# Attention feature stages of a graph transformer: 64-row projections for pairs of token tiles, and column-tiled accumulations

## What is computed

```python
Q, K, V = heads(x @ Wq + bq), heads(x @ Wk + bk), heads(x @ Wv + bv)   # 16 heads of 64
Kp = relu(normalized(K) @ projection.T) + 0.1      # 256 features a head
Qp = relu(normalized(Q) @ projection.T) + 0.1
KV = einsum('bhsf,bhsd->bhfd', Kp, V)              # 256 x 64 a head
QKV = einsum('bhsf,bhfd->bhsd', Qp, KV)
normalizer = maximum(einsum('bhsf,bhf->bhs', Qp, sum_s(Kp)), 1e-6)
out = (QKV / normalizer) @ Wo + bo
```

## Time and profile before

| | |
|---|---|
| median of 3 runs | 3448.74 us (3441.88 to 3455.16) |
| profiled execution, its own time | 3453.75 us |
| span of its trace | 3452.0 us |
| mean granted TensorE clock | 0.941 |
| TensorE / VectorE / ScalarE / GpSimd busy | 90% / 61% / 37% / 12% |
| key stage | 299.3 to 442.3 us |
| query stage | 570.3 to 714.9 us, products until 721.8 us |

### The profile page before, as it was taken

The page is one execution under the profiler, slowest core; times in us unless marked ns, Lnnn a source line. Parts: engine busy times, 40 slices in busy tenths (PEclk is TensorE's granted clock), DMA queues, the critical chain, the costliest instruction groups (busy, mean ns, idle before and its releaser), DMA issues.

```text
span 3452.0 us, 52667 instructions
## 1 busy us (share of the span) xinstructions
PE 3101.3 (90%) x21876; PEld 2834.2 (82%) x21876; DVE 2116.8 (61%) x3710; ACT 1290.2 (37%) x2211; POOL 401.6 (12%) x302
## 2 busy tenths in 40 slices
PE   6999999989998799999489999989998999969992
PEld 6897797479987398888389997989998999968882
DVE  6985377977875744434556555776264734646664
ACT  4462055544421034333244334444044413325551
POOL 1044443442000100000300000000000000010002
PEclk9999999999998899999699999999999999969996
DMA  7322123122032156534641000452321432248777
GB/s 248 106 54 40 1 62 92 1 48 68 13 88 88 46 158 190 173 128 152 187 142 38 26 27 30 122 146 76 81 88 48 115 72 81 63 133 267 258 257 228
DMA packets 284267, 366.09 MB, mean 106 GB/s; under 512 B 52472, under 2 KB 234782, under 8 KB 282224
## 3 DMA queue, kind: packets, MB, share of 16 engines
q1 hardware_dynamic: 165035, 203.54, 20.0%
q0 software_dynamic: 51248, 68.03, 8.5%
q10 hardware_dynamic: 67717, 90.69, 8.1%
HBM read 285.75 MB, written 83.74 MB: 107 GB/s over the span
## 4 chain that ended last, share of the span: by engine, by line
PE 55%; DVE 4%; DMA 2%; ACT 2%; issue 1%; ACTq 1%; POOL 1%; POOLq 0%; DVEq 0%; SPq 0%
PE PV L459 12%; PE PV L460 12%; PE PV L461 12%; PE PV L563 6%; PE PS L459 3%; PE PS L461 3%; PE PS L460 3%; DMA b<-y_d,gidx 1%; PE PA L594 1%; PE PA L487 1%; DVE b L1848 1%; DVE b_split L1634 1%; ACTq L121 1%; ACT b L1248 1%; PE PA L878 1%
## 5 line engine op out<-in xcount | busy, mean ns | idle before, releaser
L459 PE MATMUL PV<-WH,b_split 128*125 128x256 f32 (+2 forms) x3708 | 1091.1, 294 | 124.6 <-DVE b_split L1634 107.7
L460 PE MATMUL PV<-WH,b_split 128*125 128x256 f32 (+2 forms) x3708 | 1077.4, 291 | 0.0
L461 PE MATMUL PV<-WH,b_split 128*125 128x256 f32 (+2 forms) x3708 | 1076.4, 290 | 0.0
L1634 DVE TENSOR_TENSOR b_split<-b,b_split 128x500 fp32r<-128x500 f32 x1040 | 687.4, 676 | 435.5 <-ACT b_split L1237 422.4
L1237 ACT CAST b_split<-b 128x500 fp32r<-128x500 f32 x1040 | 626.0, 612 | 808.8 <-PE PV L461 733.4
L459 PEld LDWEIGHTS PV<-WH,b_split 128*125 128x125 f32 (+2 forms) x3708 | 703.6, 190 | 149.7 <-issue 105.8
L460 PEld LDWEIGHTS PV<-WH,b_split 128*125 128x125 f32 (+2 forms) x3708 | 706.5, 191 | 9.9
L461 PEld LDWEIGHTS PV<-WH,b_split 128*125 128x125 f32 (+2 forms) x3708 | 703.0, 190 | 11.3
L1617 DVE TENSOR_TENSOR WH<-WS,WH 128x1024 fp32r<-128x1024 f32 x292 | 344.3, 1221 | 145.7 <-ACT WH L1222 144.4
L1222 ACT CAST WH<-WS 128x1024 fp32r<-128x1024 f32 x292 | 292.1, 1051 | 180.4 <-PE PV L563 143.4
L459 PE MATMUL PV<-b_split,WH 128*128 128x250 f32 (+3 forms) x1136 | 336.9, 297 | 9.2 <-DVE b_split L1634 6.4
(11 more groups left out here) (271 smaller groups left out, 3775.4 us busy)
## 6 DMA issues: line engine op xcount, KB each, us to landing
WS<-in_L_ffn_w SPq DMA_DIRECT2D x46, 1024.0 KB, 6.8
WH<-at_d SPq DMA_DIRECT2D x15, 1093.8 KB
WS<-in_L_ffn_gate_w SPq DMA_DIRECT2D x16, 1024.0 KB, 5.4
WS<-in_L_ffn_up_w SPq DMA_DIRECT2D x16, 1024.0 KB, 6.1
WS<-in_L_ffn_down_w SPq DMA_DIRECT2D x16, 1024.0 KB, 5.1
y_d<-b ACTq DMA_DIRECT2D x60, 256.0 KB
y_d<-b ACTq DMA_DIRECT2D x64, 196.0 KB
b<-key_d POOLq DMA_DIRECT2D x4, 2560.0 KB, 9.4
```

Of the source, the lines that this page charges most:

```text
L459: pe.matmul(o, a[0], b[0], start=start, stop=False, **kw)
L460: pe.matmul(o, a[0], b[1], start=False, stop=False, **kw)
L461: return pe.matmul(o, a[1], b[0], start=False, stop=stop, **kw)
L1634: ve.tensor_tensor(lo, src, hi.bitcast(F32), ALU.subtract).then_inc(xl_done, 1)
```

## The change

*Key stage.* An iteration handles two token tiles of a pair of heads (40 iterations instead of 80). For each tile and head one matmul of 64 rows (partitions 0 to 63 or 64 to 127) and 256 moving columns; a bank holds one head and both tiles. The matmuls that accumulate are the same ones, eight in an iteration; they follow one iteration behind.

*Query stage.* An iteration is a step. Four projections of 64 rows go to four banks, PV 0 to 2 and PS[2] (qf_bank). ScalarE alone empties them, with one Relu each (L1479 takes 0 as the bias), into columns 1 to cn of the features. The addition of 0.1 is gone: column 0 of each of the six feature buffers is set once to 0.1 by VectorE, so the matmul's first output column holds a tenth of the sum over the features of KV, which is what the addition would have added to every column. VectorE copies this pair of columns to tenths for the first chunk of a pair of heads and adds it in the two instructions that it keeps besides the reciprocal. The accumulations become eight of 64 columns of weights: part 0 makes the results of both heads, part 1 the normalizers, and head hh writes the output partitions from 64 hh, so results and normalizers of both heads stand in matching partitions. The copies of the normalizers between partitions (L1470, L1471) are gone, and one product serves both heads.

```diff
--- before.py
+++ after.py
@@ -238,6 +239,10 @@
         def q_feats(n):
 
             return RB[:, n % 6, :] if n % 6 < 4 else WHF[:, 1, UNIT + (n % 6 - 4) * HALF:UNIT + (n % 6 - 3) * HALF]
+
+        def qf_bank(k):
+
+            return PV[:, k, :] if k < 3 else PS[:, 2, :]
 
         def q_norm(step):
 
...
@@ -720,27 +724,36 @@
             pe.wait_ge(pt_in, 16)
             pe.wait_ge(ones_col, 1)
             mark["kp"] = v.n
-            for n in range(KD * NT + 2):
-                if n < KD * NT:
-                    pr, i = divmod(n, NT)
-                    if n == KD // 2 * NT:
+            for n in range(KD * NB + 1):
+                if n < KD * NB:
+                    pr, b = divmod(n, NB)
+                    if n == KD // 2 * NB:
                         pe.wait_ge(pt_in, 32)
-                    pe.matmul(v.take(pe)[0:R, :], cols(B3)[:, pr, i * R:(i + 1) * R], proj[pr],
-                              start=True, stop=True).then_inc(v_full, 1)
-                if n >= 2:
-                    m = n - 2
-                    pr, i = divmod(m, NT)
-                    pe.wait_ge(v_free, mark["kp"] + m + 1)
-                    if i == 0 and pr >= 2:
+                    banks = v.take(pe), v.take(pe)
+                    for t in range(2):
+                        i = 2 * b + t
+                        for hh in range(2):
+                            head = slice(hh * HD, (hh + 1) * HD)
+                            mm = pe.matmul(banks[hh][0:R, t * F0:(t + 1) * F0], cols(B3)[head, pr, i * R:(i + 1) * R],
+                                           proj[pr][head, hh * F0:(hh + 1) * F0], start=True, stop=True)
+                            if t == 1:
+                                mm.then_inc(v_full, 1)
+                if n >= 1:
+                    m = n - 1
+                    pr, b = divmod(m, NB)
+                    pe.wait_ge(v_free, mark["kp"] + 2 * (m + 1))
+                    if b == 0 and pr >= 2:
                         pe.wait_ge(kv_free, 2 * (pr - 1))
-                    for hh in range(2):
-                        at = i * NH + 2 * pr + hh
-                        for f in range(2):
-                            mm = pe.matmul(kv_acc(pr)[:, hh, f * P:(f + 1) * P].rearrange("p (c d) -> p c d", c=2),
-                                           RB[0:R, m % 4, hh * F0 + f * P:hh * F0 + (f + 1) * P],
-                                           v_heads[:, at:161:160 - at, :],
-                                           start=(i == 0 and f == 0), stop=(i == NT - 1),
-                                           skip_group_check=True)
+                    for t in range(2):
+                        i = 2 * b + t
+                        for hh in range(2):
+                            at = i * NH + 2 * pr + hh
+                            for f in range(2):
+                                mm = pe.matmul(
+                                    kv_acc(pr)[:, hh, f * P:(f + 1) * P].rearrange("p (c d) -> p c d", c=2),
+                                    RB[0:R, (2 * m + hh) % 4, t * F0 + f * P:t * F0 + (f + 1) * P],
+                                    v_heads[:, at:161:160 - at, :],
+                                    start=(i == 0 and f == 0), stop=(i == NT - 1), skip_group_check=True)
                     mm.then_inc(kp_used, 1)
             pe.wait_ge(kv_free, NH)
 
@@ -750,37 +763,39 @@
             turn_heads(2 * NQ * NB - 1)
             pe.wait_ge(s_free, s.n)
 
-            mark["qp"] = v.n
-            for n in range(NH * 6 + 4):
-                if n < NH * 6:
-                    step, hh, f = n // 4, n // 2 % 2, n % 2
-                    pr, c = divmod(step, 3)
+            for n in range(KD * 3 + 1):
+                if n < KD * 3:
+                    pr, c = divmod(n, 3)
                     c0, cn = CH[c]
-                    if n == NH * 3:
+                    if n == KD // 2 * 3:
                         pe.wait_ge(pt_in, 48)
-                    if f == 0:
-                        bank, done = v.take(pe), v_full
-                    else:
-                        if n >= 2:
-                            pe.wait_ge(qa_free, n // 2)
-                        bank, done = PS[:, 2, :], qa_full
-                    at = hh * F0 + f * P
-                    pe.matmul(bank[:, 0:cn], proj[pr][:, at:at + P], cols(B3)[:, pr, c0:c0 + cn],
-                              start=True, stop=True).then_inc(done, 1)
-                if n >= 4:
-                    m = n - 4
-                    step, hh, f = m // 4, m // 2 % 2, m % 2
-                    pr, c = divmod(step, 3)
+                    for f in range(2):
+                        if n >= 1:
+                            pe.wait_ge(qf_done, 4 * (n - 1) + 2 * (f + 1))
+                        for hh in range(2):
+                            head, at = slice(hh * HD, (hh + 1) * HD), hh * F0 + f * P
+                            pe.matmul(qf_bank(2 * f + hh)[:, 0:cn], proj[pr][head, at:at + P],
+                                      cols(B3)[head, pr, c0:c0 + cn], start=True, stop=True).then_inc(qf_full, 1)
+                if n >= 1:
+                    m = n - 1
+                    pr, c = divmod(m, 3)
                     cn = CH[c][1]
-                    if f == 0:
-                        pe.wait_ge(v_free, mark["qp"] + m // 2 + 1)
-                    else:
-                        pe.wait_ge(qa_done, m // 2 + 1)
-                    if m % 4 == 0 and step >= 2:
-                        pe.wait_ge(acc_free, 2 * (step - 1))
-                    pe.matmul(q_acc(step)[:, hh, 0:cn], KV[:, 2 * pr + hh, f, :], q_feats(m)[:, 0:cn],
-                              start=(f == 0), stop=(f == 1)).then_inc(qp_used, 1)
-            pe.wait_ge(acc_free, NH * 3)
+                    if m == 0:
+                        pe.wait_ge(tenths_ready, 6)
+                    if m >= 2:
+                        pe.wait_ge(acc_free, m - 1)
+                    for f in range(2):
+                        pe.wait_ge(qf_done, 4 * m + 2 * (f + 1))
+                        for part in range(2):
+                            for hh in range(2):
+                                at = (part + hh) % 2 * HD
+                                mm = pe.matmul(q_acc(m)[hh * HD:(hh + 1) * HD, part, 0:cn + 1],
+                                               KV[:, 2 * pr + hh, f, at:at + HD],
+                                               q_feats(4 * m + 2 * f + hh)[:, 0:cn + 1],
+                                               start=(f == 0), stop=(f == 1))
+                                if part == 1:
+                                    mm.then_inc(qp_used, 1)
+            pe.wait_ge(acc_free, KD * 3)
             linear_rows("wo0")
 
 
@@ -1451,7 +1466,7 @@
             head_pieces(0)
             for h in range(NH):
                 if h % 2 == 0:
-                    act.wait_ge(kp_used, NT * (h // 2 + 1))
+                    act.wait_ge(kp_used, NB * (h // 2 + 1))
                 kvp = kv_acc(h // 2)[:, h % 2, 0:2 * P].rearrange("p (f c d) -> p f c d", f=2, c=2)
                 dst = KV[:, h, :, :].rearrange("p f (c d) -> p f c d", c=2)
                 if h % 2 == 0:
@@ -1461,28 +1476,15 @@
                     act.copy(dst[:, :, 0, :], kvp[:, :, 1, :]).then_inc(kv_free, 1)
             head_pieces(NQ * NB)
 
-            def normalisers(step):
-
-                cn = CH[step % 3][1]
-                act.wait_ge(qp_used, 4 * (step + 1))
-                if step >= 2:
-                    act.wait_ge(acc_free, 2 * (step - 1))
-                act.copy(q_norm(step)[0:64, 0:cn], q_acc(step)[64:128, 0, 0:cn]).then_inc(den_done, 1)
-                act.copy(q_norm(step)[64:128, 0:cn], q_acc(step)[0:64, 1, 0:cn]).then_inc(den_done, 1)
-
-            for n in range(1, NH * 6, 2):
-                cn = CH[n // 4 % 3][1]
-                q = q_feats(n)[:, 0:cn]
-                if n >= 6:
-                    act.wait_ge(qp_used, n - 5)
-                act.wait_ge(qa_full, n // 2 + 1)
-                act.activation(q, PS[:, 2, 0:cn], ACT.Relu).then_inc(qa_free, 1)
-                act.wait_ge(qa_free, n // 2 + 1)
-                act.activation(q, q, ACT.Copy, bias=0.1).then_inc(qa_done, 1)
-                if n >= 7 and n % 4 == 3:
-                    normalisers((n - 7) // 4)
-            normalisers(3 * KD - 1)
-            act.wait_ge(acc_free, NH * 3)
+            for n in range(KD * 3):
+                cn = CH[n % 3][1]
+                for k in range(4):
+                    if k % 2 == 0:
+                        act.wait_ge(qf_full, 4 * n + k + 2)
+                        if 4 * n + k >= 6:
+                            act.wait_ge(qp_used, 4 * n + k - 4)
+                    act.activation(q_feats(4 * n + k)[:, 1:cn + 1], qf_bank(k)[:, 0:cn], ACT.Relu).then_inc(qf_done, 1)
+            act.wait_ge(acc_free, KD * 3)
             linear_residual(B1, A["x"])
 
 
@@ -1984,35 +1986,37 @@
 
             ve.wait_ge(table_zero, 16 * NZERO)
             head_pieces(0)
```

(40 more changed lines are left out.)

10 lines of the change are left out of this document (5 added, 5 removed).

## The result

The changed kernel takes 3396.45 us (median of 4 runs, 3393.57 to 3400.18); the kernel before took 3447.21 beside it (4 runs, 3441.88 to 3455.16). The ratio is 0.9851, with a 95% interval of 0.9832 to 0.987. That is 50.8 us less. The likeliest case of the prediction was 26.5 less (3422); 52 less (3397) was the rival *Full overlap*. So nearly twice the forecast gain came. The time lies inside the stated range.

The account below looks back on a forecast made before the run. TensorE was taken to bound the key stage alone and the query stage with VectorE nearly even. Key -9.6 and query -16.9 (matmuls -14.3, end -2.6) sum to -26.5 us: 3422 off the median; range 3378 to 3455.

Parts of the forecast that it names:

- likeliest case: Both stages: staggered overlap of array halves, switches of 0 to 0.28 us; sum 26.5 us less, 3422; chance 0.50.
- Full overlap: Rival, both stages: two heads' passes always run side by side; 52 us less, 3397; chance 0.18.
- What bounds the two stages: Key stage: TensorE alone; query stage: TensorE 5.6 us a step before, VectorE 5.2; after the change 5.3 against 4.1.
- Units of a pass: TensorE in both stages: a pass takes 0.22 us for 256 columns and 0.35 for 416.
- Switches: Both stages: each change of the array's shape costs 0.2 us, two per iteration or step; ends 0 and 0.28.
- the starts of the passes: Both stages: passes start staggered in program order; 5 units for eight projection passes, 9 for sixteen accumulation passes.
- The start of the query stage: Query stage, beyond its steps: 1.75 us for first projections at half clock, about 1.3 for the wait on ScalarE.
- The end: Query stage, last matmul to last product: one VectorE step remains, 4.3 us instead of 6.9, so 2.6 less.
- ScalarE's cover: Query stage: ScalarE's second pair of Relus stays hidden with 1.2 us to spare; uncovered, each microsecond costs 24.
- Nothing is given back: After both stages: scatter chain, weight fetches and output projection take back none of the 26.5 us.
- One overlap fails: Slower rival: row halves, column halves or both don't run together; 3474, 3481 or 3533 us; chance 0.20.
- Dear switches: Rival, both stages: at 0.41 us each the 128 switches eat the 26.5; no change, 3449; chance 0.12.

Follow-up runs that it names:

- experiment 4: Changed kernel with projections and accumulations alternating tile by tile (half by half in the query stage), so twice the switches: 3416.16 us, ratio 0.9905.
- experiment 3: Changed kernel with four passes of head 0 ordered before head 1's, in key projections and query accumulations: 3392.11 us, ratio 0.9823.
- experiment 8: Changed kernel with query accumulations grouped by head over both f, eight passes of head 0 ahead: 3451.9 us in a single run.
- experiment 7: Changed kernel with the key stage in batches of two iterations, so half its switches: 3402.35 us, ratio 0.9866.
- experiment 9: Changed kernel unaltered, measured again on a third chip: 3395.23 us, ratio 0.9843.
- experiment 5: Changed kernel with both heads' projections in one half of the array (head 0 twice, output wrong): 3446.46 us in a single run.
- experiment 6: Changed kernel with query projections back on 128 rows and the block-diagonal matrix, accumulations still in column halves: 3427.06 us, ratio 0.992.

## Why the prediction was off by half

**What bounds the two stages: right.** Key stage TensorE's alone, query stage TensorE with VectorE close behind. VectorE was put at 4.1 us a step and came to about 4.1, through 0.65 instead of 0.59 twice and fewer gaps; the tenths cost 0.16 every third step. Its idle time was put at over 1 us a step and is 0.3, as the step is shorter than forecast.

**Units of a pass: right.** 0.216 us for 256 columns (0.22 forecast) and 0.351 for 416 (0.35).

**Switches: right.** 0.2 was taken, from the sum of two rows; 0.20 in either direction was measured in the key stage, by the timeline and by experiment 4. It has the two parts that the prediction named. After the last pass's 0.216 us the next load comes 0.10 us late (361.62 instead of 361.52). Then the first matmul of the new shape keeps the second from starting by 0.10 more (0.213 to the second instead of 0.11). By the Trainium skill, "TensorEngine Tiling (Array Packing)", Key Properties, a change of the tiling mode drains TensorE; the trace agrees that the change has a price: the next load comes 0.1 us late, and about as much again follows from it. The dearer end that the prediction took from that rule, 0.28, did not come.

**The step that failed: the starts of the passes.** The prediction wrote: "If the start order holds with halves too, the passes start at 0, 1, 1, 2, 2, 3, 3, 4 units". It counted 5 units for eight projection passes and 9 for sixteen accumulation passes. The passes start at 0, 0, 1, 1, 2, 2, 3, 3: 4 and 8 units. The sum made anew with these, all else as it stood:

- key iteration: 3.27 less one unit of 0.22, 3.05 (measured 3.04). Forty units of 0.22 are 8.8 us.
- query step: 5.3 less two units of 0.35, 4.6 (measured 4.56). Twenty-four times 0.7 are 16.8 us.

Together 25.6, the whole distance between the forecast (-26.5) and the rival (-52). The rival's own sum came close: -18.4 for -17.6 in the key stage and -33.8 for -33.9 in the query stage. The latter is luck in part, as 1.1 us too little for the matmuls and 1.0 too much for the end cancel in it. The mechanism, two halves at once against two changes of shape, was the forecast one; only this term's size was wrong. The prediction had taken the order of records on an undivided array, where it is plain, for a rule between halves, where no row showed it. Experiments 3 and 8 show that it is none. That an overlap was there at all had no row behind it either: it was a choice between two bounds, and the runs put it at the upper one. By the Trainium skill, "TensorE: Matmul & The Clock Gate", The mechanism, matmuls of several tiles start in program order some nanoseconds apart, and its drawing lets them run side by side. The small distance agrees (5 to 14 ns). The order does not: in experiment 8 the fifth matmul of a step starts before the fourth. The forecast had read the order and let the drawing go.

**The start of the query stage: near.** Its start at half clock and the wait on ScalarE were put at 3 us beyond the steps; 112.2 - 24 x 4.56 = 2.8. The granted clock was 0.69 over the first ten us (0.83 before).

**The end: 1.0 us short.** 4.3 forecast, 5.3 measured. The sum started from a VectorE that is idle when the last matmul ends. But the last step's accumulations follow directly on those of the step before, 3.0 us, and VectorE needs 4.1 for that step. This is an oversight of its own: with the forecast's 9 units the accumulations would have taken 3.15 us, still less than 4.1.

**ScalarE's cover: right.** 1.2 us to spare were forecast, and 1.1 are there (604.15 to 605.23). Experiment 8 shows the price once the cover is gone: 0.45 us of its step of 6.45.

**Nothing is given back: right.** The output projection starts as long after VectorE's end as before (5.3 us), and the scatter chain, though it ends 13 us later than before, is done over 70 us before the counts are read. That time can be won or lost in the experts' code with the place of the code (7 us against the kernel before, 16 between experiments 7 and 9) was in no term of the sum.

**One overlap fails, Dear switches:** refuted by experiments 5, 6 and 4. Experiment 5 is the world in which row halves don't overlap, and the forecast for it was fair: key 3.93 an iteration against 3.04 + 0.86 = 3.90 measured. But the slower side had been given 0.20, on an argument ("this trace has no overlap of matmuls") that was absence of evidence: the trace before held no half-array instruction at all.

## What to carry to other kernels

Two heads with 64 rows (or 64 columns) each run at full overlap in the two halves of the array when their instructions alternate at least every four passes. Count pairs, not a stagger, and 0.15 to 0.2 us for each change of shape, so put as much work as the banks allow between changes. A block-diagonal operand on the whole array gives that half away (experiment 6: 2.99 us instead of 1.60). After such a gain look at what is next (here VectorE, 4.1 of 4.56 us), and when a stage's gain does not reach the end, look for idle time at branches before doubting the stage.

## What the runs showed of the hardware that was not expected

- Passes on different halves start 5 to 7 ns apart, ahead of the earlier half's second pass, and 14 ns apart where four passes of one half stand first.
- The look-ahead ends at four passes of a busy half, in rows and in columns: with eight ahead the other half starts with the fifth, 1.46 us late with passes of 0.35 (606.784 against 605.327), 0.97 late with passes of 0.216 (364.262 against 363.292).
- A change of shape between 64-row matmuls and the others costs 0.15 to 0.20 us: 0.10 before the first load, the rest (0.05 or 0.10) between the first and the second matmul.
- Thirty-eight instructions more or fewer, 700 us earlier, decide over some 10 us of idle time at five places in the experts' code, four of them behind a branch, and over 14 to 16 us of time there (329.3 and 329.0 us against 312.5, 313.0 and 314.8). One of the branches takes 1.2 or 6.8 us by it. What makes it so stays open.
